# The norm stage of a graph layer: variances node by node, their roots turned into rows by TensorE, and the recurrence's input kept as three float32 rests

## The reference, cut to what matters

```python
xn = _layernorm(x, axis=-1)
x = x + _L0_gnn_ref(xn, src, dst, ...) + _L0_mix_ref(xn[None], ...)[0]
x = x + _L0_ffn_ref(_layernorm(x, axis=-1)[None], ...)[0]

def _layernorm(x, axis=-1, eps=1e-05):
    m = jnp.mean(x, axis=axis, keepdims=True)
    v = jnp.var(x, axis=axis, keepdims=True)
    return (x - m) / jnp.sqrt(v + eps)
```

## Time and profile before

| | us |
|---|---|
| median of 3 runs (lowest, highest) | 17174.56 (17168.83, 17176.53) |
| the profiled execution's own time | 17166.22 |
| its span, on which every row below stands | 17164.5 |
| norm stage, window 3837 to 4070 | 233 |
| LSTM stage, window 4070 to 17000 | 12930 |

### The profile page before, as it was taken

The page is one execution under the profiler, slowest core; times in us unless marked ns, Lnnn a source line. Parts: engine busy times, 40 slices in busy tenths (PEclk is TensorE's granted clock), DMA queues, the critical chain, the costliest instruction groups (busy, mean ns, idle before and its releaser), DMA issues. The chain is left out here.

```text
span 17164.5 us, 921688 instructions
## 1 busy us (share of the span) xinstructions
PE 12677.3 (74%) x375188; PEld 11671.1 (68%) x375188; DVE 10168.9 (59%) x84253; ACT 5191.2 (30%) x32399; POOL 2587.7 (15%) x1609
## 2 busy tenths in 40 slices
PE   1333344456888888888888888888888888888886
PEld 1222233345888888888888888888888888888885
DVE  2333211127666666666666666666666666666666
ACT  0000000023333333333333333333333333333332
POOL 0888888810000000000000000000000000000000
PEclk5666666675555555555555555555555555555555
DMA  3444444420000000000000000000000000000000
GB/s 103 71 72 72 68 68 68 68 74 23 1 1 1 1 1 1 1 1 1 1 1 1 1 1 1 1 1 1 1 1 1 1 1 1 1 1 1 1 1 16
DMA packets 938625, 317.06 MB, mean 18 GB/s; under 512 B 750941, under 2 KB 908138, under 8 KB 938596
## 3 DMA queue, kind: packets, MB, share of 16 engines
q0 software_dynamic: 435200, 207.54, 8.0%
q1 hardware_dynamic: 503396, 109.17, 3.2%
HBM read 150.06 MB, written 150.93 MB: 18 GB/s over the span
## 5 line engine op out<-in xcount | busy, mean ns | idle before, releaser
L1231 PE MATMUL bank<-hrest,whh 128*128 128x1 bf16 (+1 forms) x300000 | 9078.1, 166 | 1907.0 <-DVE hrest L1355 1907.0
L1231 PEld LDWEIGHTS bank<-hrest,whh 128*128 128x128 bf16 x300000 | 8554.3, 104 | 2467.4 <-DVE hrest L1355 2466.9
L1299 ACT ACTIVATE gates<-bank 128x4 f32<-128x4 f32 x12500 | 2179.9, 174 | 8140.1 <-DVE bank L1336 7251.3
L1336 DVE TENSOR_REDUCE bank<-bank 128x4 f32<-128x12 f32 x12500 | 2208.7, 177 | 3190.3 <-PE bank L1231 2303.3
L1231 PE MATMUL bank<-xsteps,wih 128*128 128x15 bf16 (+1 forms) x60048 | 2716.0, 175 | 0.0
L1344 DVE CUSTOM_DVE_ANT_1 uv<-gates 128x4 f32<-128x4 f32 x12500 | 2034.4, 163 | 456.3
L1231 PEld LDWEIGHTS bank<-xsteps,wih 128*128 128x128 bf16 x60048 | 2279.6, 104 | 0.0
L1307 ACT ACTIVATE bank<-gates 128x1 f32<-128x1 f32 x12500 | 2176.2, 174 | 131.6
L1360 DVE TENSOR_TENSOR hrest<-hrest 128x1 f32<-128x1 f32 x12500 | 1986.6, 159 | 216.2
L1365 DVE TENSOR_TENSOR hrest<-hrest 128x1 f32<-128x1 f32 x12500 | 1959.2, 157 | 217.1
L1231 PE MATMUL bank<-ones,gbias 128*128 128x5 bf16 x10008 | 1679.0, 168 | 18.5 <-DMA xsteps<-x_d 18.5
(11 more groups left out here) (170 smaller groups left out, 3784.4 us busy)
## 6 DMA issues: line engine op xcount, KB each, us to landing
ht<-acc_d SPq DMA_DIRECT2D x100, 250.0 KB
xsteps<-x_d SPq DMA_DIRECT2D x1252, 7.5 KB, 1.7
U<-hrest SPq DMA_DIRECT2D x1250, 5.0 KB, 1.7
acc_d<-zero SPq DMA_DIRECT2D x24, 796.9 KB
rows<-xn_d,staged_i POOLq DMA_INDIRECT x800, 4.0
acc_d<-sums,target POOLq DMA_INDIRECT x800, 6.1
x_d<-x SPq DMA_DIRECT2D x25, 375.0 KB, 2.3
xall<-in_x SPq DMA_DIRECT2D x5, 1250.0 KB
```

The lines of the kernel that those rows point to most:

```text
L1231: return nc.tensor.matmul(to, w, v, start=start, stop=True, skip_group_check=True)
L1299: nc.scalar.activation(gates[:, k, 0:2 * NG_[k]:2], zi[k], ACT.Tanh).then_inc(ifg_act[k], 1)
L1336: nc.vector.tensor_reduce(zi[k], gi[k][b][:, s], axis=AX.X, op=ALU.add).then_inc(ifg_summed[k], 1)
```

## The change

The variances are formed node by node: the squares become the weights and one column of `avg` the moving operand, so that 125 nodes land on 125 partitions, one number each, two such columns to a chunk. The epsilon, the root, the reciprocal and the Newton step work on 125x2 numbers. PE then turns the two columns of inverse roots into 250-wide rows that all 128 partitions hold, by a transposition of a column repeated 128 times (`root_rows`, banks 3 and 4). DVE multiplies `cent` with these rows into part 0 of `x2`, now float32; part 1 is part 0 minus its own upper half read as bf16, part 2 the same of part 1. ACT takes no part in the split any more. `x2`, `x2_d` and `xsteps` double in bytes, and their order becomes part, feature half, node. The LSTM's projection reads the upper halves, 40 bytes from one part to the next and 4 from one node to the next, parts innermost. All of DVE's, ACT's and PE's steps are rearranged: the small instructions of chunk c+1 stand between the large ones of chunk c.

```diff
-    x2_d = nc.dram_tensor("x2_d", (128, (NB + 2) * KD * B * PARTS), BF16, kind="Internal").ap()
+    x2_d = nc.dram_tensor("x2_d", (128, (NB + 2) * KD * B * PARTS), F32, kind="Internal").ap()
...
-            cvar, croot, crs, ctmp = (sb(n, [128, C], F32, st) for n in ("cvar", "croot", "crs", "ctmp"))
-            xl = sb("xl", [128, KD, C], F32, st)
-            res = sb("res", [128, KD, C], F32, st)
-            x2 = sb("x2", [128, 2, C // B, KD, B, PARTS], BF16, st)
+            nvar, nroot, nrs, nsq, nfix = (sb(n, [R, 2, 2], F32, st) for n in ("nvar", "nroot", "nrs", "nsq", "nfix"))
+            x2 = sb("x2", [128, 2, C // B, PARTS, KD, B], F32, st)
+            x2_hi = x2[:].bitcast(BF16).rearrange("p b n c k (t e) -> p b n c k t e", e=2)
...
             def part(b, p):
-                return x2[:, b, :, :, :, p].rearrange("p n k t -> p k n t")
-
-
+                return x2[:, b, :, p, :, :].rearrange("p n k t -> p k n t")
+
+            def part_hi(b, p):
+                return x2_hi[:, b, :, p, :, :, 1].rearrange("p n k t -> p k n t")
...
                 def variance(c):
                     pe.wait_ge(csq_ready, c + 1)
                     if due(c):
-                        pe.wait_ge(rs_ready, c)
-                    for k in range(KD):
-                        last = nc.tensor.matmul(bank[2][:, 0:C], avg[:], csq[:, k, :], start=k == 0, stop=k == KD - 1)
+                        pe.wait_ge(nvar_ready, c)
+                    for j in range(2):
+                        for k in range(KD):
+                            last = nc.tensor.matmul(bank[2][0:R, j:j + 1], csq[:, k, j * R:(j + 1) * R], avg[:, 0:1],
+                                                    start=k == 0, stop=k == KD - 1)
                     last.then_inc(var_made, 1)
 
+                def root_rows(c, b):
+                    pe.wait_ge(nrs_ready, c + 1)
+                    if due(c - 1):
+                        pe.wait_ge(p1_ready, c - 1)
+                    for j in range(2):
+                        last = nc.tensor.transpose(bank[3 + b][:, j * R:(j + 1) * R],
+                                                   nrs[:, b, j:j + 1].broadcast_to([R, 128]), ident[0:R, 0:R])
+                    last.then_inc(rows_made, 1)
+
                 def step(c, n, b):
+                    root_rows(c, b)
+                    if within(c + 3):
+                        mean(c + 3, 1 - b)
                     if within(c + 2):
-                        mean(c + 2, b)
-                    if within(c + 1):
-                        variance(c + 1)
+                        variance(c + 2)
 
                 mean(0, 0)
                 mean(1, 1)
                 variance(0)
+                mean(2, 0)
+                variance(1)
                 skewed(pe, step)
...
-                def second_part(c, b):
-                    act.wait_ge(r1_ready, c + 1)
-                    nc.scalar.activation(part(b, 1), by_block(res[:]), ACT.Copy).then_inc(p2_ready, 1)
+                def root(c, b):
+                    act.wait_ge(nvar_ready, c + 1)
+                    nc.scalar.activation(nroot[:, b, :], nvar[:, b, :], ACT.Sqrt).then_inc(nroot_ready, 1)
 
                 def step(c, n, b):
-                    act.wait_ge(rs_ready, c + 1)
-                    nc.scalar.activation(croot[:], cvar[:], ACT.Sqrt).then_inc(croot_ready, 1)
-                    if within(c - 1):
-                        second_part(c - 1, 1 - b)
                     if within(c + 1):
-                        square(c + 1, 1 - b)
-                    act.wait_ge(xl_ready, c + 1)
-                    if due(16 * n):
-                        act.wait_ge(x2_out[b], 16 * n)
-                    nc.scalar.activation(part(b, 0), by_block(xl[:]), ACT.Copy).then_inc(p1_ready, 1)
-                    if within(c + 3):
-                        batch_norm(c + 3)
+                        root(c + 1, 1 - b)
+                    if within(c + 2):
+                        square(c + 2, b)
+                    if within(c + 4):
+                        batch_norm(c + 4)
...
-                        dve.wait_ge(xl_ready, c - 1)
+                        dve.wait_ge(p1_ready, c - 1)
...
+                def variance(c, b):
+                    dve.wait_ge(var_made, c + 1)
+                    nc.vector.tensor_scalar(nvar[:, b, :], bank[2][0:R, 0:2], LN_EPS, None, ALU.add)\
+                      .then_inc(nvar_ready, 1)
+
+                def inverse(c, b):
+                    dve.wait_ge(nroot_ready, c + 1)
+                    if due(c - 1):
+                        dve.wait_ge(rows_made, c - 1)
+                    nc.vector.reciprocal(nrs[:, b, :], nroot[:, b, :]).then_inc(nrs0, 1)
+
+                def inverse_square(c, b):
+                    dve.wait_ge(nrs0, c + 1)
+                    nc.vector.tensor_tensor(nsq[:, b, :], nrs[:, b, :], nrs[:, b, :], ALU.mult).then_inc(nsq_ready, 1)
+
+                def correction(c, b):
+                    dve.wait_ge(nsq_ready, c + 1)
+                    nc.vector.scalar_tensor_tensor(out=nfix[:, b, :], in0=nsq[:, b, :], scalar=-0.5, in1=nvar[:, b, :],
+                                                   op0=ALU.mult, op1=ALU.mult).then_inc(nfix_ready, 1)
+
+                def corrected(c, b):
+                    dve.wait_ge(nfix_ready, c + 1)
+                    nc.vector.scalar_tensor_tensor(out=nrs[:, b, :], in0=nfix[:, b, :], scalar=1.5, in1=nrs[:, b, :],
+                                                   op0=ALU.add, op1=ALU.mult).then_inc(nrs_ready, 1)
+
+                def scaled(c, n, b):
+                    rows_ = bank[3 + b][:, 0:C].rearrange("p (o n t) -> p o n t", o=1, t=B)\
+                        .broadcast_to([128, KD, C // B, B])
+                    dve.wait_ge(rows_made, c + 1)
+                    if due(16 * n):
+                        dve.wait_ge(x2_out[b], 16 * n)
+                    nc.vector.tensor_tensor(part(b, 0), cent[:, b].rearrange("p k (n t) -> p k n t", t=B), rows_,
+                                            ALU.mult).then_inc(p1_ready, 1)
+
                 def first_rest(c, b):
-                    dve.wait_ge(xl_ready, c + 1)
                     dve.wait_ge(p1_ready, c + 1)
-                    if due(c):
-                        dve.wait_ge(p2_ready, c)
-                        dve.wait_ge(p3_ready, c)
-                    nc.vector.tensor_tensor(by_block(res[:]), by_block(xl[:]), part(b, 0), ALU.subtract)\
-                      .then_inc(r1_ready, 1)
-
-                def third_part(c, b):
-                    dve.wait_ge(r1_ready, c + 1)
+                    nc.vector.tensor_tensor(part(b, 1), part(b, 0), part_hi(b, 0), ALU.subtract).then_inc(p2_ready, 1)
+
+                def second_rest(c, b):
                     dve.wait_ge(p2_ready, c + 1)
-                    nc.vector.tensor_tensor(part(b, 2), by_block(res[:]), part(b, 1), ALU.subtract)\
-                      .then_inc(p3_ready, 1)
+                    nc.vector.tensor_tensor(part(b, 2), part(b, 1), part_hi(b, 1), ALU.subtract).then_inc(p3_ready, 1)
 
                 def step(c, n, b):
-                    dve.wait_ge(var_made, c + 1)
-                    nc.vector.tensor_scalar(cvar[:], bank[2][:, 0:C], LN_EPS, None, ALU.add).then_inc(rs_ready, 1)
+                    more = within(c + 1)
+                    if more:
+                        variance(c + 1, 1 - b)
+                    if within(c + 3):
+                        residual(c + 3)
+                    if more:
+                        inverse(c + 1, 1 - b)
+                    scaled(c, n, b)
+                    if more:
+                        inverse_square(c + 1, 1 - b)
                     if within(c + 2):
-                        residual(c + 2)
-                    if within(c - 1):
-                        first_rest(c - 1, 1 - b)
-                    if within(c + 1):
-                        center(c + 1, 1 - b)
-                    dve.wait_ge(rs_ready, c + 1)
-                    dve.wait_ge(croot_ready, c + 1)
-                    done = [0]
-
-                    def link(ins):
-                        done[0] += 1
-                        ins.then_inc(norm_chain, 1)
-                        dve.wait_ge(norm_chain, REFINE_STEPS * c + done[0])
-
-                    refine_rsqrt(nc, link, crs[:], croot[:], cvar[:], ctmp[:])
-                    if within(c - 1):
-                        third_part(c - 1, 1 - b)
-                    if due(c):
-                        dve.wait_ge(p1_ready, c)
-                        dve.wait_ge(r1_ready, c)
-                    rs2 = crs[:].rearrange("p (o n) -> p o n", o=1).broadcast_to([128, KD, C])
-                    nc.vector.tensor_tensor(xl[:], cent[:, b], rs2, ALU.mult).then_inc(xl_ready, 1)
+                        center(c + 2, b)
+                    if more:
+                        correction(c + 1, 1 - b)
+                    first_rest(c, b)
+                    if more:
+                        corrected(c + 1, 1 - b)
```

(17 more changed lines are left out.)

19 lines of the change are left out of this document (10 added, 9 removed).

## The result

The changed kernel takes 17075.16 us (median of 4 runs, 17071.35 to 17076.09) against 17174.17 before on the same chip: a ratio of 0.9941 with an interval of 0.9929 to 0.9953, 99.0 us saved. The prediction said 17072, 102 saved. The profiled execution took 17071.35, its span is 17069.6.

What follows compares the result with a forecast made beforehand. Each norm-stage chunk was bound by DVE's list (about 7.1 us) plus 2.04 waiting for ACT. Intervals saving 99.9 and the end 2.5 gave 102.4: 17174.6 - 102.4 = 17072 us, range 17042 to 17107.

Steps and rivals of the forecast that it cites:

- The ring: Norm stage: `nvar`, scaling, centre, square, PE's variance set each chunk, 5.25 us, taken as 5.05; chance 0.56.
- A sixth of the stage at 2.4 GHz: PE's clock in the norm stage: a sixth at the high level, where the ring is near 4.1 us, giving 5.05.
- The variance: PE, norm stage: four matmuls, eight records with float32 loads 0.20 us apart, 1.97 us; high end 2.9, low end 1.15.
- The writes: DVE, norm stage: three float32 results written to `x2` in runs of five, 0.67 to 0.70 us each; high end 1.25.
- rival B: Norm stage: float32 writes at 1.25 us or a variance of 2.9, or both; total 17085 to 17107 us; chance 0.19.
- DVE's list: DVE, per norm-stage chunk: five large and five small instructions, 3.45 us, ending near 3.9, then idle over 1 us.
- Fill, tail, DMA: Norm stage: filling changes by 0, within 2 us; the end saves 2.5; `x2` out lands in 3.3 us, hidden.
- The sum: Norm stage: 24 intervals from 219.0 to 119.1 us, saving 99.9; the end saves 2.5; in all 102.4.
- The LSTM's operand: LSTM projection's strided read of `xsteps`: costs 0, covered by PE's idle 0.30 us up to 27 ns more per product.
- Rival D: LSTM: strided read lengthens each projection product, slower than before; at eight times per column about 17510 us; chance 0.04.
- C: Norm stage: PE at 2.4 GHz through most of it, chunk 4.0 to 4.4 us, total 17047 to 17056; chance 0.15.
- E: LSTM: each step 11 to 22 ns longer through reads of the same memory, total 17141 to 17210 us; chance 0.06.

Runs made afterwards that it cites:

- variance_twice: The changed kernel with the four variance products of each chunk issued twice: 17110.8 us, ratio 0.9950 to the kernel before.
- deeper: The unrolled kernel with three buffers of `cent` instead of two, residual and batch norm one chunk further ahead: 17059.94 us, ratio 0.9923 to the kernel before.
- unrolled: The changed kernel with the norm stage's 25 chunks written out, without the hardware loop: 17077.98 us against 17084.59 for the changed kernel.
- parts_adjacent: The changed kernel with the three float32 parts of a value side by side in `x2` and `xsteps`: 17087.61 us against 17084.59 for the changed kernel.
- bf16_runs: The kernel before with bf16 `x2` and `xsteps` parts outermost, written in runs of five: 17173.4 us against 17194.5, ratio 0.9987.
- after_again: The changed kernel itself, unaltered, on the chip of unrolled, deeper and parts_adjacent: 17084.59 us against 17188.13 for the kernel before there.

## Why the prediction was right

**The ring.** It is the one that was named. The waits name it, variance_twice shows that PE's variance is on it, and deeper, where the centre no longer stands behind the scaling and the chunk falls to 3.66, that it closes there. The forecast of 5.05 us stood on an error and one that offset it:

- At 1.2 GHz the ring was said to be 5.25. The unrolled chunks take 4.78. The scaling starts 0.74 behind `nvar` (3951.66, 3952.40) and not 1.03, because the rows are not on the ring. The earlier trace rows were read as two transpositions, 1.19 us; they are four (the output stage turns two feature halves of two groups of nodes at a time), and two are two records, 0.66 us in all. That is 0.29. The square starts earlier behind the centre (0.71 for 0.79) and is 0.62 long for 0.66: 0.12. The variance takes 1.84 for 1.97: 0.13. The second small instruction stands between scaling and centre: 0.06 the other way.
- A sixth of the stage at 2.4 GHz was assumed. The granted clock is 0.51 over the stage and 0.50 in the unrolled kernel from 3860 to 3940. Only the fill and the first chunk stand higher: 0.65 in the window below, 0.60 from 3850 to 3855, and 0.50 from there on. From 3860 to 3940 PE is busy 88% of the time in the changed kernel and stays at 0.50. So next to nothing of the chunks ran at the upper level:

```profile
3842.00:3850.00 8.00, 5.87 (x20) 4.20 (x20) 3.65 (x8) 4.00 (x9) 0.00 (x0) 0.65 0.01 3
```

- The loop's own instructions were left out: 4.94 and 5.04 instead of 4.78. The ring was 0.47 too long, the clock took 0.20 off it, and the loop adds 0.2; that 5.05 lies so near to the loop's 4.99 is in part luck.

The three together leave 24 intervals in 115.7 us where 119.1 were said. The last interval is 2.4 instead of 3.0.

**The variance.** 1.97 from the float32 loads' spacing in the earlier trace rows, 1.84 measured; eight loads span 1.75. By the Trainium skill ("TensorE: Matmul & The Clock Gate", section on LDWEIGHTS) the estimate was 1.3; the trace of the changed kernel does not agree, its loads of 125 float32 columns follow each other at 0.2 us and not at 0.1. The measurement decides, and the row of the same trace was the better guide.

**The writes.** Taken at 0.67 to 0.70, measured 0.65 to 0.68; the doubt about them (rival B) was settled by the runs of five. The reason given (the pattern of addresses alone doesn't cost, since a read with six bytes' step takes 0.67) was wrong: parts_adjacent pays 0.2 for a float32 write every 12 bytes, and bf16_runs shows that the 1.25 of the third part was the six-byte step. It holds for reads; for writes the step costs.

**DVE's list.** 0.15 to 0.17 for a small instruction and 0.6 from one large one to the next, as taken: it ends 3.8 us behind `nvar`, where 3.9 was said. The text ahead of the prediction says that no instruction but the centre waits for one of the two large ones ahead of it. That is wrong for both rests: L1135 waits for the scaling, L1139 for L1135 right ahead of it, and starts 0.70 behind it (3908.08, 3908.78). It costs the ring nothing, since DVE is idle behind it.

**Fill, tail, DMA.** Fill 1.3 us less where 0 was taken, tail 2.6 less where 2.5 was; the transfer of 750 KB lands in 3.2 us where 3.3 was said, hidden.

**The sum.** The stage gained 107.2, said 102.4: 3.4 from the intervals, 1.3 from the fill. The profiled executions gained 94.9, since their other stages stand 12.3 us longer, within their own movement, and the medians 99.0 on this chip and 103.5 on that of after_again. That the median came within 3 us of the forecast is in part luck.

**The LSTM's operand.** 0 was taken. A 15-column product is 180 ns for 179, the step 2.05 to 2.06, ten steps 20.61 to 20.63 us in both kernels, PE's idle time 0.29 for 0.30; parts_adjacent, without the jumps of 40 bytes, has an LSTM no shorter. Rival D is out: the reading costs nothing, so the cover (0.44 us, not 0.30) was not needed. The Trainium skill's note on cachelines ("SBUF — State Buffer", section on the DMA port swizzle) agrees in sign with DVE's slower writes every 12 bytes (0.86 for 0.65), and no run here shows such a cost for PE's reads. The bf16 write every six bytes has two or three numbers to a line and costs more still (1.25 for 0.73), as the prediction noted; the measurement decides.

**The other rivals.** B (dearer parts) and C (2.4 GHz through the stage) are out by the rows above. E (a step longer by 11 ns or more, 0.11 in ten steps) is out by the 20.62 us of ten steps in both kernels; why they are 20.66 in another execution, nothing in the traces tells.

## What to carry to other kernels

When two parts of a change remove the same wait, their gains don't add: time each alone, or follow the ring and see which wait is left. After such a change look for what closes the new ring; here it was the centre behind the scaling, and a third buffer, with another order and one chunk more of lead, gave 23 us of the unrolled stage's 128. Count the records of an operation at one known place before taking its time from a group: the transpositions were taken at nearly double their time (1.19 us for 0.66) by an error of counting.

## What the runs showed of the hardware

- DVE writes 500 numbers per partition in 0.67 us in float32 and 0.73 in bf16, both in runs of five; in 0.86 to 0.89 in float32 every 12 bytes, and in 1.25 in bf16 every six bytes. ACT's bf16 copy: 0.78 in runs, 1.30 every six bytes.
- A hardware loop of two chunks costs 0.16 to 0.26 us a chunk on DVE, on the path.
- Eight loads of 125 float32 columns follow each other at 0.20 us at a granted clock of 0.50, a bf16 load of 128 columns is 0.10 long. Two float32 transpositions take 0.66 us.
- PE stayed at a granted clock of 0.50 while busy in all of 40 us (deeper).
- 14 more products in each LSTM step cost 33 us in all by the medians (50.5 by the profiles), with 20 more PE stops for 4.4 and 2.1 us in every second pass of the loop, 3035 us in all; the cause is open.
- The same kernel's LSTM and output took 13096.0 us in one profile and 13120.4 in another: ten steps are 20.62 or 20.63 us in the one and 20.65 to 20.68 in the other, from start to end.
